# Mixing and expert kernel, one core: a first pair of eight plain products, and mixing weights built from a table on the chip

## The chip, the cores and the metric

One Trainium2 chip, one core of it. The metric is the device time of one execution in microseconds (us), lower is better. The kernel before takes 992.26 us, the median of three runs (991.84 to 992.67).

## The reference, cut to what matters

```python
# x (128, 64, 1024), cond (128, 128), all float32
h = gelu(cond @ W0 + b0); h = gelu(h @ W1 + b1)
att = softmax(h @ W2 + b2)                     # (128, 8)
agg_w = einsum('bk,koi->boi', att, weight)     # one 64x64 mixing matrix for each of 128 batches
z = einsum('boi,bih->boh', agg_w, x) + (att @ bias_k)[:, :, None]
base = z @ base_W.T                            # 1024 x 1024
probs = softmax(z @ router_W.T)                # 8 experts, the best 2, renormalised: w_dense
mid = einsum('bsd,edr->bser', z, lora_A) * w_dense[..., None]      # rank 16 for each expert
out = x + base + einsum('bser,erd->bsd', mid, lora_B) * 2
```

## The kernel before, in words

Two batches make a tile of 128 rows, two tiles of such a kind a pair; there are 32 pairs. For a pair, TensorE first mixes: with `mix_w` (128x128, two 64x64 matrices on the diagonal, one for each batch) it multiplies 16 chunks of x into `y_ps` (`mix_chunk`, L476), and VectorE adds the bias and writes `ya` (`add_bias`, L850). `ya` holds four blocks of 128x512: A11, A21 (first half of the columns), A12 and A22 (second half), where the first index is the set of rows and the second the half of the 1024 columns.

The large product with `base_W` is 2x2 blocks of 1024x1024 halves, and each block product would be eight of them. The kernel uses a rule with seven products: GpSimd makes sums of the blocks of `ya` (S1 to S4: L366, L374, L380, L383), and at the start sums of the weights (T1 to T4, from the blocks B11, B12, B21, B22). Every operand, of data and of weights, is split into a high part (ScalarE: `split_high` L711, `take_hi` L658) and the rest (VectorE: `split_low` L859, `take_lo` L802), and a product is three matmuls for each of four chunks: high by high, high by low, low by high. Four of the seven products carry the router and `lora_A` columns beside them (`product_with_side`, L515 and L518: 12 pairs of matmuls of 376 and 272 columns), three don't (`product`, L504: 12 matmuls of 512 columns).

A tile's routing is a chain of twelve small operations on VectorE with one exponential on ScalarE (L864 to L898), which ends in `mid`. TensorE transposes `mid` into `pd` (`transpose_mid`, L526), ScalarE and VectorE split it (L722, L905), and three matmuls for each half of the columns add `mid` times `lora_B` (`up`, L536). The second tile's `mid` of a pair is used in the next pair, inside its first product. Results gather in `out_sb` (VectorE L910, GpSimd L405), and SyncE stores them and loads x and the residual.

The order on each engine is written out by hand (`body` on every engine, semaphores between them); `over_pairs` runs pairs 0 and 1 unrolled, then a loop of two pairs a turn, then the last two unrolled. In the steady pairs the first four products have the 16 mixing chunks of the next pair between their matmuls (`mixed_in`).

The mixing matrices of all batches but the first four come by way of DRAM: eight matmuls over the kernels' weights (`mixing_kernels`, L432) give all 128x4096 values, ScalarE copies them (`take_agg`, L663) into `agg`, one DMA writes `agg` to DRAM, and four DMAs a pair (L268, 16 KB each in pieces of 128 bytes) bring two 64x64 matrices for each tile into `mix_w`. For the first pair alone, VectorE multiplies a table `mix_i` (128x512: 64 outputs by 8 kernels) by the attention weights (L827), sums over the 8 kernels (L831), and ScalarE places the result (`place_mix`, L672).

## Time and profile before

| what | value |
|---|---|
| median of the runs | 992.26 us (991.84 to 992.67) |
| profiled execution | 992.38 us, of which the span from first to last instruction is 990.6 us |
| granted TensorE clock, mean | 0.989 |
| busy: TensorE, VectorE, GpSimd, ScalarE | 963.9, 686.5, 330.5, 208.7 us |
| DMA | 115.00 MB in 64145 packets, 38392 of them under 512 bytes |

A row of the timeline gives the start, the length of one or of several merged operations, the engine, the line and what is written from what, and in brackets the idle time before it with what ended it. PE is TensorE, DVE VectorE, ACT ScalarE, POOL GpSimd, SP SyncE. "x2" on a float32 matmul counts its two passes.

### The profile page before, as it was taken

The numbers are of one execution on the slowest core, as the hardware profiler recorded it, in microseconds if no ns is written. First come the engines' busy times: TensorE is split into PE (matmuls) and PEld (weight loads), VectorE is DVE, ScalarE is ACT, GpSimd is POOL, SyncE is SP. The second block draws the span as 40 slices with busy tenths as digits, with TensorE's granted clock in tenths as the row PEclk, the third lists the DMA queues.
The fourth block names the chain that finished last, engine by engine and source line by source line (L and its number), as shares of the span: only waits on it lengthen the run. The fifth ranks groups of instructions, "written<-read, shape, count | busy, mean of one in ns | idle before, by whom it ended". The sixth has DMA issues, their size and how long they took to land.

```text
span 990.6 us, 17707 instructions
## 1 busy us (share of the span) xinstructions
PE 963.9 (97%) x5742; PEld 882.8 (89%) x5742; DVE 686.5 (69%) x1529; ACT 208.7 (21%) x422; POOL 330.5 (33%) x245
## 2 busy tenths in 40 slices
PE   6788999999999999999999999999999999999998
PEld 4577999999999999999999999999999999999996
DVE  2878676677676667767667776766776766677674
ACT  3432121122211211212121121211212112122120
POOL 4904333322333322333332233333223333223331
PEclk9889999999999999999999999999999999999999
DMA  8324333433423333332343333334333233433311
GB/s 281 100 122 136 103 106 115 135 108 111 128 93 114 120 132 111 112 113 93 114 135 117 116 122 101 105 114 135 109 111 133 90 115 117 134 109 112 120 48 54
DMA packets 64145, 115.00 MB, mean 116 GB/s; under 512 B 38392, under 2 KB 38520, under 8 KB 63480
## 3 DMA queue, kind: packets, MB, share of 16 engines
q1 hardware_dynamic: 63856, 114.76, 35.0%
q8 instruction: 9, 0.15, 0.1%
q10 hardware_dynamic: 272, 0.03, 0.0%
q14 instruction: 8, 0.07, 0.0%
HBM read 79.01 MB, written 35.68 MB: 116 GB/s over the span
## 4 chain that ended last, share of the span: by engine, by line
PE 91%; issue 4%; POOL 2%; DMA 1%; DVE 1%; SPq 0%; POOLq 0%; DVEq 0%
PE pc L504 17%; PE pa L515 13%; PE pb L515 13%; PE y_ps L476 11%; PE pb L518 9%; PE pa L518 9%; PE pd L504 9%; PE pc L536 4%; PE pd L536 4%; DMA c_raw<-in_base_t 1%; PE pd L526 1%; POOL w_raw L360 1%; POOL w_raw L348 1%; POOL lb_lo L395 0%; DVE out_sb L910 0%
## 5 line engine op out<-in xcount | busy, mean ns | idle before, releaser
L405 POOL TENSOR_TENSOR out_sb<-out_sb,u 128x512 f32<-128x512 f32 x96 | 136.4, 1451 | 209.1 <-DVE u L956 209.1
L476 PE MATMUL y_ps<-mix_w,x_sb 128*128 128x128 f32 x1024 | 199.5, 280 | 0.7 <-issue 0.7
L476 PEld LDWEIGHTS y_ps<-mix_w,x_sb 128*128 128x128 f32 x1024 | 171.9, 194 | 17.3 <-issue 3.9
L366 POOL TENSOR_TENSOR ya<-ya 128x512 f32<-128x512 f32 x32 | 42.6, 1331 | 420.7 <-DVE ya L850 420.7
L850 DVE TENSOR_TENSOR ya<-y_ps,bias_sb 128x512 f32<-128x512 f32 x128 | 87.7, 686 | 34.4 <-PE y_ps L476 31.3
L504 PE MATMUL pc<-w_hi,s_hi 128*128 128x512 f32 x256 | 106.8, 417 | 2.9 <-DVE out_sb L910 2.9
L515 PE MATMUL pa<-w_hi,a_hi 128*128 128x376 f32 x256 | 101.5, 397 | 6.2 <-DVE w_lo L802 6.2
L504 PE MATMUL pc<-w_hi,s_lo 128*128 128x512 f32 x256 | 101.2, 395 | 0.0
L504 PE MATMUL pc<-w_lo,s_hi 128*128 128x512 f32 x256 | 100.5, 393 | 0.0
L515 PE MATMUL pa<-w_lo,a_hi 128*128 128x376 f32 x256 | 86.3, 337 | 0.0
L515 PE MATMUL pa<-w_hi,a_lo 128*128 128x376 f32 x256 | 86.2, 337 | 0.0
L715 ACT ACTIVATE exps<-logits,neg_max 128x8 f32<-128x8 f32 x64 | 19.3, 301 | 300.0 <-DVE neg_max L867 300.0
L722 ACT ACTIVATE mid_hi<-pd 128x128 fp32r<-128x128 f32 x64 | 17.7, 277 | 292.1 <-PE pd L526 292.1
L859 DVE TENSOR_TENSOR a_lo<-ya,a_hi 128x512 fp32r<-128x512 f32 x96 | 69.4, 723 | 8.3 <-ACT a_hi L711 8.3
L518 PE MATMUL pa<-w_hi,a_hi 128*128 128x272 f32 x256 | 74.2, 290 | 0.0
L518 PE MATMUL pa<-w_lo,a_hi 128*128 128x272 f32 x256 | 74.2, 290 | 0.0
L518 PE MATMUL pa<-w_hi,a_lo 128*128 128x272 f32 x256 | 74.0, 289 | 0.0
L910 DVE TENSOR_TENSOR out_sb<-pc,out_sb 128x512 f32<-128x512 f32 x96 | 65.7, 684 | 1.0 <-POOL out_sb L405 0.6
L504 PE MATMUL pd<-w_hi,s_hi 128*128 128x512 f32 x128 | 61.6, 481 | 4.4 <-DVE w_lo L802 4.4
L711 ACT ACTIVATE a_hi<-ya 128x512 fp32r<-128x512 f32 x96 | 60.2, 627 | 25.0 <-DVE ya L850 25.0
L504 PEld LDWEIGHTS pc<-w_hi,s_hi 128*128 128x128 f32 x256 | 48.5, 190 | 14.1 <-issue 3.3
L515 PEld LDWEIGHTS pa<-w_hi,a_hi 128*128 128x128 f32 x256 | 49.5, 193 | 9.8 <-issue 7.0
(149 smaller groups left out, 2373.6 us busy)
## 6 DMA issues: line engine op xcount, KB each, us to landing
x_sb<-in_x SPq DMA_DIRECT2D x64, 512.0 KB, 3.4
out_sb<-in_x SPq DMA_DIRECT2D x64, 512.0 KB, 4.3
out<-out_sb SPq DMA_DIRECT2D x64, 512.0 KB, 2.8
bias_sb<-bias_rows SPq DMA_DIRECT2D x62, 64.0 KB, 5.2
agg_rows<-agg SPq DMA_DIRECT2D x1, 2048.0 KB, 9.1
...
```

The source lines that it names most:

```text
L366: nc.gpsimd.tensor_tensor(y_block(0, 1), y_block(0, 1), y_block(0, 0), ALU.subtract).then_inc(s3_set, 1)
L405: nc.gpsimd.tensor_tensor(o, o, u2[:, :], ALU.add).then_inc(done, 1)
L476: mm = nc.tensor.matmul(y_ps[q % 2][:, j * P:(j + 1) * P], x_sb[m][:, c * P:(c + 1) * P], mix_w[m][:, :], start=True, stop=True)
L504: mm = nc.tensor.matmul(to[:, 0:BANK], y[o][:, j * P:(j + 1) * P], w[:, at:at + BANK], start=(begin and j == 0 and n == 0), stop=(j == HAL ...
L515: nc.tensor.matmul(to[:, LEAD:BANK], y[o][:, j * P:(j + 1) * P], w[:, at:at + HEAD], start=start, stop=stop, skip_group_check=True)
L518: mm = nc.tensor.matmul(to[:, BANK:BANK + 2 * SD].rearrange("p (a n) -> p a n", a=2), y[o][:, j * P:(j + 1) * P], tail, start=start, stop= ...
L536: mm = nc.tensor.matmul(to[:, :], m[:, :], w[:, cols], start=(begin and n == 0), stop=(n == 2), skip_group_check=True)
L711: nc.scalar.activation(op_hi[o][:, :], OPERAND[o], ACT.Copy).then_inc(op_hi_set[o], 1)
L715: nc.scalar.activation(exps[:, :], logits[:, :], ACT.Exp, bias=neg_max[:, :]).then_inc(exps_ready, 1)
L850: nc.vector.tensor_tensor(to[:, :, :, m, :], y_ps[q % 2][:, :].rearrange("p (j s r) -> p j s r", j=HALF, s=2), bias_sb[m][:, :].rearrange( ...
L859: nc.vector.tensor_tensor(op_lo[o][:, :], OPERAND[o], op_hi[o][:, :].bitcast(f32), ALU.subtract).then_inc(op_lo_set[o], 1)
L910: nc.vector.tensor_tensor(o, src, o, ALU.add).then_inc(done, 1)
```

## The change

The first pair no longer uses the seven-product rule: its four blocks are made with eight products (`first_pair` on TensorE: A11 and A21 by B11, A12 and A22 by B21, A11 by B12, A12 by B22, A21 by B12, A22 by B22), so it needs neither the sums of its data nor T1 to T4. Its mixing chunks for the second pair, its two transposes of `mid` and all four `up` steps lie inside it, so the second pair has none of the `up` steps of a pair before it. T1 to T4 are all made by GpSimd, in quarters of 128x512, for the second pair.

The mixing matrices no longer come from DRAM. One matmul of 512 columns puts the attention weights of all tiles on every partition (`att_rows`). For each later tile one operation multiplies the table `mix_i` by them (`scale_mix`), VectorE sums over the 8 kernels (`sum_mix`), and ScalarE places the result with two copies (`place_mix`). For tiles of the second and third pair VectorE multiplies too; from there on GpSimd does. `mixing_kernels`, `take_agg`, `agg` and its DMAs are gone, the start's loads have another order, and the idle transposes of the start are replaced by float32r matmuls of 512 columns (`hot`). The steady pairs' products on TensorE stay as they were.

Cut to its core:

```diff
             sp.dma_start(mlp[:, :], params).then_inc(params_in, 16)
-            sp.dma_start(b2_sb[:, :], b2.partition_broadcast(P)).then_inc(b2_in, 16)
+            sp.dma_start(mix_i[:, :], mix_t).then_inc(mix_i_in, 16)
+            sp.dma_start(bk_sb[:, :], bias_k).then_inc(bk_in, 16)
             sp.dma_start(a_raw[:, :], base_t[0, :, :]).then_inc(a_in, 16)
-            for b in range(PAR):
-                sp.dma_start(mix_i[b * C:(b + 1) * C, :], mix_t).then_inc(mix_i_in, 16)
-            sp.dma_start(bk_sb[:, :], bias_k).then_inc(bk_in, 16)
-            for m in range(2):
-                sp.dma_start(x_sb[m][:, :], x_t[m, :, :]).then_inc(x_in[m], 16)
-            sp.dma_start(mix_k[:, :], mix_rows).then_inc(mix_k_in, 16)
+            sp.dma_start(x_sb[0][:, :], x_t[0, :, :]).then_inc(x_in[0], 16)
             sp.dma_start(w_raw[W_SIDE], side).then_inc(side_in, 16)
+            sp.dma_start(x_sb[1][:, :], x_t[1, :, :]).then_inc(x_in[1], 16)
+            sp.dma_start(b_raw[:, :], base_t[2, :, :]).then_inc(b_in, 16)
             sp.dma_start(c_raw[:, :], base_t[1, :, :]).then_inc(c_in, 16)
             sp.dma_start(d_raw, base_t[3, :, :]).then_inc(d_in, 16)
-            sp.dma_start(b_raw[:, :], base_t[2, :, :]).then_inc(b_in, 16)
             sp.dma_start(lb_raw[:, :], lora_b.rearrange("e r d -> (e r) d")).then_inc(lb_in, 16)
...
-            def mixing_weights(t, m, rows):
-                for b in range(PAR):
-                    dst = mix_w[m][b * C:(b + 1) * C, :].rearrange("i (s b c) -> i s b c", s=2, b=PAR)
-                    r = PAR * t + b
-                    if rows is agg:
-                        src = agg[r:r + 1, :].rearrange("b (i s c) -> b i s c", i=C, s=2)
-                    else:
-                        src = agg_dram[r, :].rearrange("(i s c) -> i s c", i=C, s=2)
-                    sp.dma_start(dst[:, :, b, :], src).then_inc(mix_w_in[m], 16)
+                             ).then_inc(bias_in[m], 16)
...
+            def make_t3(n):
+                nc.gpsimd.tensor_tensor(w_raw[t_piece(T3, n)], c_raw[quarter(n)], w_raw[t_piece(B22, n)],
+                                        ALU.subtract).then_inc(t3_made, 1)
...
+            def scale_mix(n, m, to):
+                pool.wait_ge(summed_set, 2 * n + m)
+                nc.gpsimd.tensor_tensor(to[:, :].rearrange("p (c k) -> p c k", k=K),
+                                        mix_i[:, :].rearrange("p (c k) -> p c k", k=K),
+                                        att_rows[:, bass.ts(2 * n + m, K)].unsqueeze(1).broadcast_to([P, C, K]),
+                                        ALU.mult).then_inc(scaled_set, 1)
...
             def body(p, k):
+                if mixes_after(p):
+                    pool.wait_ge(op_lo_set[S1], p)
+                    scale_mix(p + 2, 0, s1)
                 if not last(p):
-                    sums(p + 1)
+                    sum_s3(p + 1)
+                if mixes_after(p):
+                    scale_mix(p + 2, 1, s1)
...
-                    nc.tensor.transpose(pb[:, 0:P], ident[:, :], ident[:, :])
-            def mixing_kernels(n):
...
+                    nc.tensor.matmul(pb[:, 0:BANK], hot[:, 0:P], hot[:, :], start=True, stop=True)
...
             pe.wait_ge(att_t_ready, 1)
             nc.tensor.matmul(bias_ps, att_t[:, :], bk_sb[:, :], start=True, stop=True).then_inc(bias_mm, 1)
+            keep_warm(1)
...
-                if q < 3:
-                    mixing_kernels(q + 1)
-            pe.wait_ge(agg_act, 2)
-            pe.wait_ge(side_lo_set, 1)
+                if q == 1:
+                    pe.wait_ge(spread_set, 1)
+                    nc.tensor.matmul(pb[:, BANK:], parity[:, :], att_spread[:, :], start=True,
+                                     stop=True).then_inc(att_rows_mm, 1)
...
+            def plain(hi, lo, high_w, low_w, to, j, begin):
+                cols = slice(j * BANK, (j + 1) * BANK)
+                for n, (y, w) in enumerate(((hi, high_w), (hi, low_w), (lo, high_w))):
+                    mm = nc.tensor.matmul(to[:, 0:BANK], y[:, j * P:(j + 1) * P], w[:, cols],
+                                          start=(begin and j == 0 and n == 0), stop=(j == HALF - 1 and n == 2),
+                                          skip_group_check=True)
+                return mm
...
+                for j in range(HALF):
+                    wait_low(w_lo_set[B11], j)
+                    plain_with_side(*a11, B11, pa, j, 0, True)
+                pe.wait_ge(a21_hi_set, 1)
+                pe.wait_ge(a21_lo_set, 1)
+                pe.wait_ge(att_rows_set, 1)
+                for j in range(HALF):
+                    plain_with_side(*a21, B11, pb, j, 0, True)
+                wait_operand(A12, 0)
+                for j in range(HALF):
+                    wait_low(w_lo_set[B21], j)
+                    mm = plain_with_side(*a12, B21, pa, j, 1, False)
+                mm.then_inc(c11_mm, 1)
+                wait_operand(A22, 0)
+                for j in range(HALF):
+                    mm = plain_with_side(*a22, B21, pb, j, 1, False)
+                    if j == HALF - 1:
+                        mm.then_inc(c21_mm, 1)
+                    mix_chunk(1, 0, j)
+                for j in range(HALF):
+                    wait_low(b12_lo_set, j)
+                    mm = plain(*a11, *b12, pc, j, True)
+                    if j == HALF - 1:
+                        mm.then_inc(p1_mm, 1)
+                    mix_chunk(1, 1, j)
+                transpose_mid(0)
+                for j in range(HALF):
+                    wait_low(w_lo_set[B22], j)
+                    mm = plain(*a12, *b22, pc, j, False)
+                    if j == HALF - 1:
+                        mm.then_inc(p2_mm, 1)
+                    mix_chunk(1, 2, j)
+                pe.wait_ge(lb_lo_set, 1)
+                wait_mid(0)
+                plain_up_base(0, pa)
+                up(1, pc, False, plain_up)
+                transpose_mid(1)
+                for j in range(HALF):
+                    mix_chunk(1, 3, j)
+                wait_mid(1)
+                for j in range(HALF):
+                    mm = plain(*a21, *b12, pd, j, True)
+                mm.then_inc(a21_mm, 1)
+                for j in range(HALF):
+                    mm = plain(*a22, *b22, pd, j, False)
+                mm.then_inc(p4_mm, 1)
+                plain_up_base(0, pb)
+                up(1, pd, False, plain_up)
...
+            def place_mix(n, m):
+                act.wait_ge(summed_set, 2 * n + m + 1)
+                if first(n):
+                    act.wait_ge(zeros_set, 4)
+                else:
+                    act.wait_ge(mixed, 4 * n + m - 1)
...
+                if mixes_after(p):
+                    for m in range(2):
+                        place_mix(p + 2, m)
...
+            def sum_mix(n, m, of):
+                dve.wait_ge(scaled_set, 2 * n + m + 1)
+                if not first(n):
+                    dve.wait_ge(mix_set[m], PAR * n)
+                nc.vector.tensor_reduce(summed[m][:, :], of[:, :].rearrange("p (c k) -> p c k", k=K), AX.X,
+                                        ALU.add).then_inc(summed_set, 1)
...
+            def first_pair():
+                add_bias(0, 0)
+                add_bias(0, 1)
+                split_low(A11, 0)
+                low_side()
+                dve.wait_ge(a21_hi_set, 1)
+                nc.vector.tensor_tensor(a21_lo[:, :], y_block(0, 1), a21_hi[:, :].bitcast(f32),
+                                        ALU.subtract).then_inc(a21_lo_set, 1)
+                add_bias(0, 2)
+                add_bias(0, 3)
+                split_low(A12, 0)
+                split_low(A22, 0)
                 for n in range(WP):
                     take_lo(B21, n)
-                dve.wait_ge(t3_made, WP)
+                dve.wait_ge(att_rows_set, 1)
+                for m in range(2):
+                    scale_mix(1, m, scaled)
+                    sum_mix(1, m, scaled)
+                dve.wait_ge(t1_made, TP)
+                dve.wait_ge(t3_made, TP)
                 for n in range(WP):
-                    take_lo(T3, n)
-                dve.wait_ge(t2_made, WP)
-                for n in range(WP):
-                    take_lo(T1, n)
-                dve.wait_ge(p2_mm, 1)
+                    dve.wait_ge(b12_hi_set, n + 1)
+                    nc.vector.tensor_tensor(b12_lo[half_block(n)], c_raw[half_block(n)],
+                                            w_hi[w_piece(T4, n)].bitcast(f32), ALU.subtract).then_inc(b12_lo_set, 1)
+                dve.wait_ge(c11_mm, 1)
                 route_logits(0, pa[:, SLOG])
                 route_choice(0)
                 route_weigh(0, pa[:, SMID])
-                split_low(S2, 0)
-                dve.wait_ge(t4_made, WP)
+                dve.wait_ge(t2_made, TP)
+                for n in range(WP):
+                    take_lo(B22, n)
+                add_bias(1, 0)
+                dve.wait_ge(lb_hi_set, 1)
+                nc.vector.tensor_tensor(lb_lo[:, :], lb_raw[:, :], lb_hi[:, :].bitcast(f32),
+                                        ALU.subtract).then_inc(lb_lo_set, 1)
+                dve.wait_ge(c21_mm, 1)
+                route_logits(1, pb[:, SLOG])
+                route_choice(1)
+                route_weigh(1, pb[:, SMID])
+                split_mid(0)
+                add_bias(1, 1)
+                for n in range(WP):
+                    take_lo(T3, n)
+                split_low(A11, 1)
+                add_bias(1, 2)
+                dve.wait_ge(plain_up, 2)
+                dve.wait_ge(res_in[0][0], 16)
+                add_into(0, 0, 0, pa[:, BASE], plain_out)
+                split_mid(1)
+                add_into(0, 0, 1, pc[:, :], plain_out)
+                split_low(S3, 1)
+                add_bias(1, 3)
+                for n in range(WP):
+                    take_lo(T1, n)
+                split_low(A12, 1)
+                for m in range(2):
+                    scale_mix(2, m, scaled)
+                    sum_mix(2, m, scaled)
+                dve.wait_ge(t4_made, TP)
                 for n in range(WP):
                     take_lo(T2, n)
-                add_p7(0, 0)
-                split_low(S1, 0)
-                make_u2(0)
-                split_low(A22, 0)
-                for n in range(WP):
-                    take_lo(T4, n)
-                split_mid(0)
-                add_bias(1, 0)
...
+                if mixes:
+                    sum_mix(p + 2, 0, s1)
...
+                if mixes:
+                    sum_mix(p + 2, 1, s1)
                 make_u2(p)
                 if mixing:
```

In `body`, GpSimd's queue in the loop. Before, one pair:

```order
L366 TENSOR_TENSOR ya<-ya 128x512 [waits y_ready]
L403 ISA [waits out22_p7,u2_ready]
L405 TENSOR_TENSOR out_sb_73<-out_sb_73,u_77 128x512 [waits res_in01]
L405 TENSOR_TENSOR out_sb_72<-out_sb_72,u_77 128x512 [waits res_in00]
L405 TENSOR_TENSOR out_sb_73<-out_sb_73,u_77 128x512 [waits res_in01]
```

and in the change (`s_56` is S1's buffer, which the products of the table borrow):

```order
L416 TENSOR_TENSOR s_56<-mix_i,att_rows 128x512
L389 ISA
L390 TENSOR_TENSOR ya<-ya 128x512 [waits y_ready]
L415 REGISTER_ALU
L416 ISA [waits summed_set]
L416 TENSOR_TENSOR s_56<-mix_i,att_rows 128x512
L426 ISA [waits out22_p7,u2_ready]
L428 TENSOR_TENSOR out_sb_73<-out_sb_73,u_77 128x512 [waits res_in01]
```

One product stands ahead of the sum S3 (L390) and one right behind it, ahead of the three additions into `out_sb`.

VectorE's queue in the loop, in the change, between the first tile's routing and `u2`:

```order
L1049 TENSOR_TENSOR mid<-pa,gate 128x128 [waits mid_tr,route_step]
L1010 TENSOR_TENSOR a_lo<-ya,a_hi 128x512 [waits op_hi_set0]
L1086 ISA [waits p7_mm]
L1061 TENSOR_TENSOR out_sb_73<-pb,out_sb_73 128x512 [waits res_in01]
L984 REGISTER_ALU
L1001 TENSOR_TENSOR ya<-y_ps,bias_sb_80 128x4x2x64 [waits op_lo_set6,op_lo_set2,mixed]
L1010 TENSOR_TENSOR s_lo<-ya,s_hi 128x512 [waits op_hi_set3]
L928 REGISTER_ALU
L931 TENSOR_REDUCE summed_103<-s_56 128x64 [waits mix_set1,scaled_set]
L1096 TENSOR_TENSOR u_77<-pd,p_76 128x512 [waits u2_in21,p1_kept,p6_mm]
```

The second sum over kernels (L931) is new, right ahead of `u2` (L1096); the first one stands behind the rests of A22 and S4.

TensorE's queue in the first pair, in the change, where A11 by B12 ends and A12 by B22 begins:

```order
L496 MATMUL y_ps<-mix_w_79,x_sb_54 128x128
L569 MATMUL pd<-ident,mid 128x128 [waits route_step]
L561 MATMUL pc<-w_hi,a_hi 128x512 [waits w_lo_set6]
L561 MATMUL pc<-w_lo,a_hi 128x512
L561 MATMUL pc<-w_hi,a_lo 128x512
L496 MATMUL y_ps<-mix_w_78,x_sb_53 128x128 [waits y_ready]
```

The transpose of the first tile's `mid` (L569) stands ahead of the sixth product, and waits for the whole routing chain.

## Rows read from the trace of the kernel before

**Rows 1.** The page's part 1: busy time of each engine.
```profile
PE 963.9 (97%) x5742; PEld 882.8 (89%) x5742; DVE 686.5 (69%) x1529; ACT 208.7 (21%) x422; POOL 330.5 (33%) x245
```
**Rows 2.** Chain of work that ended last: start, us, what (the ends of two pairs).
```profile
113.06 0.70 PE pc L536 x3
...
957.83 0.70 PE pc L536 x3
```
**Rows 3.** Windows: length, busy time of PE, PEld, DVE, ACT, POOL, PEclk, DMA share, GB/s.
```profile
15.00:31.00 16.00, 16.00 (x46) 9.80 (x45) 4.29 (x5) 4.79 (x10) 8.37 (x5) 1.00 0.62 246
31.00:46.00 15.00, 8.82 (x36) 6.34 (x36) 14.14 (x7) 10.42 (x14) 15.00 (x7) 0.81 0.35 114
56.00:83.50 27.50, 20.76 (x99) 17.98 (x100) 20.85 (x40) 9.01 (x14) 5.42 (x4) 0.81 0.11 35
500.00:529.13 29.13, 29.13 (x180) 27.01 (x180) 20.40 (x48) 5.85 (x12) 9.42 (x7) 1.00 0.36 115
```
**Rows 4.** Waits of TensorE: us in total, times, longest.
```profile
PE pa L515 <- DVE w_lo L802: 6.2, 1, 6.2
PE pd L504 <- DVE w_lo L802: 4.4, 1, 4.4
PE pa L432 <- DMA mix_k<-in_mix_rows: 3.5, 1, 3.5
PE pc L504 <- DVE out_sb L910: 2.9, 1, 2.9
```
**Rows 5.** Timeline of TensorE, 0 to 90 us.
```profile
14.02 2.07 PE L432 MATMUL pa<-mix_k,att_t 8*128 8x512 f32 x2 [3.53 <-DMA mix_k<-in_mix_rows]
16.02 1.97 PE L459 MATMUL pd<-bias_rows_sb,pick_row 128*128 128x64 f32 x8
17.78 2.02 PE L476 MATMUL y_ps<-mix_w,x_sb 128*128 128x128 f32 x8
...
31.47 0.66 PE L515 MATMUL pa<-w_hi,a_hi 128*128 128x376 f32 x1
...
33.24 0.44 PE L515 MATMUL pa<-w_hi,a_hi 128*128 128x376 f32 x1
...
83.58 0.34 PE L515 MATMUL pa<-w_hi,a_hi 128*128 128x376 f32 x1
```
**Rows 6.** Timeline of VectorE, 0 to 90 us.
```profile
11.10 0.69 DVE L831 TENSOR_REDUCE summed<-scaled 128x64 f32<-128x512 f32 x1
...
32.47 5.68 DVE L920 TENSOR_TENSOR w_raw<-c_raw,w_raw 128x1024 f32<-128x1024 f32 x2
...
58.47 2.35 DVE L802 TENSOR_TENSOR w_lo<-w_raw,w_hi 128x1024 fp32r<-128x1024 f32 x2
```
**Rows 7.** Timeline of GpSimd, 0 to 90 us.
```profile
18.42 2.35 POOL L348 TENSOR_TENSOR w_raw<-c_raw,a_raw 128x1024 f32<-128x1024 f32 x1 [2.24 <-DMA c_raw<-in_base_t]
...
37.02 6.09 POOL L360 TENSOR_TENSOR w_raw<-b_raw,w_raw 128x1024 f32<-128x1024 f32 x2
```
**Rows 8.** Timeline of VectorE in one steady pair, 500 to 530 us.
```profile
504.14 1.19 DVE L876 TENSOR_TENSOR beats<-ties,earlier 128x64 f32<-128x64 f32 x1
...
510.82 0.69 DVE L956 TENSOR_TENSOR u<-pd,p 128x512 f32<-128x512 f32 x1 [1.29 <-PE pd L504]
...
517.81 0.73 DVE L864 COPY logits<-side_b 128x8 f32<-128x8 f32 x1
...
521.95 0.68 DVE L910 TENSOR_TENSOR out_sb<-pd,out_sb 128x512 f32<-128x512 f32 x1
```
**Rows 9.** Timeline of GpSimd in that pair.
```profile
503.92 1.33 POOL L366 TENSOR_TENSOR ya<-ya 128x512 f32<-128x512 f32 x1 [13.22 <-DVE ya L850]
...
517.22 1.29 POOL L380 TENSOR_TENSOR s<-s,ya 128x512 f32<-128x512 f32 x1
```
**Rows 10.** Timeline of TensorE in that pair: two transposes of `mid`.
```profile
512.92 0.27 PE L526 MATMUL pd<-ident,mid 128*128 128x128 f32 x1
...
523.65 0.27 PE L526 MATMUL pd<-ident,mid 128*128 128x128 f32 x1
```

547 lines of the change are left out of this document (297 added, 250 removed).

## The prediction

> **What bounds the kernel now.** I read the busy times first, then the chain of waits, then the windows, then the timelines of the first 90 us. TensorE is busy 97% of the span and VectorE 69% [rows 1]. The chain shows the same step, the last `up` of a pair, at 113.06 and at 957.83 us, 29 pairs apart: (957.83 - 113.06) / 29 = 29.13 us a pair [rows 2]. The window over one such pair has TensorE busy for all of its 29.13 us at the high clock, 2.4 GHz (granted clock 1.00) [rows 3]. So a steady pair is TensorE's own work, and no change in it helps unless matmuls go; there the change takes none away. What can be won lies ahead of 113.76 us, where the third pair begins. The second pair begins at 83.58 us [rows 5], so the start and the first pair take almost three pairs' time. There TensorE waits 3.5 us for `mix_k`, 6.2 us for the low part of B21, 4.4 us for that of T2 and 2.9 us for an addition into `out_sb` [rows 4]; between 31 and 46 us VectorE is busy 14.1 of 15 us and GpSimd all 15 [rows 3]. The first pair is bound by these two, which make sums and low parts of weights.
>
> **The start.** Before, TensorE waits for `mix_k` until 14.02 us, then runs the first of its matmuls (2.07 us), the eight passes of the bias (1.97 us), and four blocks of mixing of 2.02 us with three more `mix_k` matmuls between them, up to 31.47 us [rows 5]. The change drops these four and the wait. The matmul before the wait ends at 14.02 - 3.53 = 10.5 us; ScalarE's copy of the bias rows puts the bias passes at 11.0. Then come 1.97 us for them, about 0.9 for two wake-up matmuls (estimate, 1024 columns at 1.2 GHz), 8.1 for mixing, and 2.07 for the matmul that spreads the attention weights (512 columns of float32, as `mix_k`). The first product starts at about 24.0 us, 7.5 earlier. Its low parts are not later: the second block of mixing is done at 18, and VectorE needs three operations after it.
>
> **The first pair on TensorE.** It has the work of a steady pair, 29.13 us, plus one product without side columns (12 matmuls at 0.70 / 3 = 0.23 us [rows 2], 2.8 us), plus 0.4 us for `up` steps cut in two: 32.3 us at the high clock. Of it 13.7 us stand behind the first transpose of `mid`: three products (8.3), four `up` steps (3.2), and half of the mixing (eight chunks; four take 2.02 us at 1.2 GHz [rows 5], so 2.0 at 2.4) with a transpose (0.2). So 18.6 us stand ahead of it, and TensorE could be there at 24.0 + 18.6 + 0.9 (the first chunk runs at the low clock, 31.47 to 33.24 [rows 5]) = 43.5 us.
>
> **The first pair on VectorE, which I take to set its time.** A low part of 1024 columns takes 2.35 / 2 = 1.18 us alone and 5.68 / 2 = 2.84 us beside GpSimd's sums, and such a sum takes 2.35 alone and 3.05 beside VectorE [rows 6, 7]. So the two slow each other when both read operands in SBUF. The change gives GpSimd 16 sums of 512 columns (about 1.2 us alone, half of 2.35) without a pause from when B12 lands, near 18 us as before [rows 7], to about 45 us. I price VectorE's operations beside them at 0.6 + 1.1 = 1.7 us for 512 columns and 1.2 + 1.1 = 2.3 for 1024. From 18.6 us it has, ahead of the end of the first tile's routing: six operations of 512 columns (10.2), five of 1024 or 1088 (11.5: side columns, B21, B12), two bias additions and two sums over kernels (2.6; 0.69 each [rows 6]), and the routing (2.6 alone, 5 with waits). That is 29.3 us: `mid` is ready near 48 us, and TensorE, due at 43.5, waits some 4 us in front of the transpose. Behind it VectorE has the low part of B22, a bias addition and lora_B's low part (4.3), the second routing and the first split (2.9), then a bias addition, T3, A11, another bias addition and an addition into `out_sb` (5.4 with one contended), before the second split at about 61 us, for which TensorE waits ahead of the seventh product. Behind that come two products and two `up` steps, 7.1 us. The second pair starts near 67.5 us, with the low clock after the waits in it in part (a window with such waits has a mean of 0.81 [rows 3]).
>
> **The second pair.** 29.13 less two `up` steps and a transpose (1.6) is 27.5 us. Those steps had covered ScalarE's copy of P1, which now stands behind two high parts of T4; I add 1.9 us for it, 0.6 for mixing weights that VectorE finishes late, and 0.7 for the unexplained rest of a first pass through the code. The third pair starts at 98.2 us against 113.76: 15.6 us earlier.
>
> **The steady pairs.** Removed: four DMAs of 16 KB a pair, which nobody waits for. Added on VectorE: two sums of 0.6 us, start to start. Added on GpSimd: two products of 512 columns, no row of their own; S3 is the nearest, 1.33 us [rows 9], and that is my price; the bounds are 1.2 and 2.7 us (twice S3, should the repeated operand halve the rate). ScalarE's four copies fit in its pause (busy 5.85 of 29.13 us [rows 3]). Which waits could become late? The product behind S3 holds VectorE's routing for about 0.65 us more (S3 already holds it: 1.19 us for an operation on 64 columns [rows 8]). With the second sum, `u2` is ready 1.25 us later; before, VectorE stood idle 1.29 us just there [rows 8], so `u2` stays at 511.5 us, and the transpose that needs it runs at 512.92 [rows 10]. The second transpose needs an addition into `out_sb` that ends at 522.6 and runs at 523.65 [rows 8, 10]: slack of 1.0 us. I cost the steady pairs at nothing; the cover is those 1.3 and 1.0 us.
>
> **Sum.** The profiled execution took 992.4 us (span 990.6); less 15.6 is 976.8. The median of the runs is 0.1 lower, so 976.7 us. Differences below 0.2%, 2 us, can't be told from none here.
>
> **A rule against the change.** VectorE's COPY of 8 columns began at 517.81 and took 0.73 us, until 518.54, and GpSimd's sum ran from 517.22 to 518.51 [rows 8, 9]: the copy waited out the whole operation. The Trainium skill (SBUF — State Buffer, Who interferes with whom) has it as an exclusive lock held for a full instruction, and says that `tensor_reduce` never contends on this chip. By that rule the two new sums are free of it, and the first pair's operations wait somewhat longer than my 1.1 us; the sum would come to about 979.
>
> **Rivals.** (1) *Each pair loses (slower).* The product right behind S3 and the second sum delay `u2`, with it GpSimd's three additions and S2, S1, S4, and these then meet the second routing, where S1 and S4 already hold it (0.73 for a copy [rows 8]). Price at the worst: a product of 2.7 instead of 1.33 (+1.4), the sums 1.2, the first product's share 0.65 and one more operation of 1.3 in the second routing, 4.6 us against covers of 1.3 + 1.0: 2.3 us a pair, 67 us over 29 pairs. It decides against the change from 15.6 / 29 = 0.54 us a pair; at 0.8 us a pair the time is 1000. For it speaks that the cover is used up almost exactly; against it that the second cover comes behind the first. Chance 0.07. The first product starts at 18 to 19 us; VectorE then sets the rest, and only 3 to 5 us come of it: 972.5. Chance 0.13. (4) *The start gains, the first pair doesn't*: GpSimd and VectorE block each other for longer (2.8 us for each operation as in [rows 6]): 11 operations by 0.8 more, plus the low clock, 12 us: 989. Chance 0.05. The forecast has 0.58.
>
> **Numbers.** The likely case spans 973 to 980. The range takes in rival 3 and most of rival 2: 970 to 985. Faster by over 0.2%: 0.58 + 0.13 + 0.16 + 0.04 = 0.91; within 0.2%: 0.02; slower: 0.07.
>
> **What would show it.** Right: the first product at 22 to 25 us; the longest waits of TensorE in the first pair in front of the transpose (on `mid`) and of the seventh product (on the low part of `mid`); the second pair at 66 to 69 us, the third at 96 to 100; steady pairs of 29.13 us. Wrong: a steady pair above 29.3 us with TensorE waiting for VectorE, GpSimd's product above 2 us, or a first product at 30 us.

## The result, and the profile after

The changed kernel took 974.95 us, median of 4 runs (974.58 to 976.25), beside 992.46 us of the kernel before in the same job (991.84 to 993.33). The ratio is 0.9825, with a 95% interval from 0.9808 to 0.9842: 17.5 us less, where the prediction had 15.6 less, 976.7 us in a range of 970 to 985. The profiled execution spans 972.9 us, 17.7 less than 990.6.

Busy times of the page, part 1, of the changed kernel:

```profile
PE 953.7 (98%) x5747; PEld 878.3 (90%) x5747; DVE 742.1 (76%) x1592; ACT 231.5 (24%) x537; POOL 402.5 (41%) x305
```

Against [rows 1] VectorE has 55.6 us more to do, GpSimd 72, and the time fell all the same. Where it fell is shown by the chain of waits (start, us, what):

```profile
92.55 2.75 PE pc L524 x12
121.69 2.75 PE pc L524 x12
...
500.37 2.75 PE pc L524 x12
529.51 2.75 PE pc L524 x12
```

From 529.51 back to 121.69 are 14 pairs: 407.82 / 14 = 29.13 us a pair, as in [rows 2]. Nothing was won or lost in the steady pairs. The windows of the first rows' stretches (length, busy time of PE, PEld, DVE, ACT, POOL, PEclk, DMA share, GB/s) show the rest:

```profile
15.00:31.00 16.00, 13.86 (x93) 12.73 (x92) 14.07 (x12) 8.50 (x12) 14.17 (x8) 1.00 0.76 275
31.00:46.00 15.00, 9.91 (x63) 8.97 (x61) 14.59 (x19) 6.13 (x10) 14.43 (x10) 0.99 0.00 1
56.00:83.50 27.50, 24.45 (x142) 22.28 (x142) 26.91 (x42) 8.13 (x16) 9.27 (x6) 0.94 0.52 158
500.00:529.13 29.13, 29.13 (x180) 27.00 (x179) 22.22 (x50) 6.71 (x16) 11.86 (x10) 1.00 0.32 113
```

VectorE now has work for 14.07, 14.59 and 26.91 us of the first three windows; it had it for 4.29, 14.14 and 20.85 [rows 3]. TensorE's longest waits (us in total, times, longest):

```profile
PE pd L569 <- DVE mid L1049: 5.0, 1, 5.0
...
PE pd L561 <- DVE mid_lo L1056: 2.4, 1, 2.4
PE pa L549 <- DVE w_lo L914: 1.1, 1, 1.1
...
PE pa L535 <- ACT p L834: 0.7, 1, 0.7
```

The waits for `mix_k`, for T2 and for the addition into `out_sb`, and most of that for B21 [rows 4], are gone. In the first pair there stand in their place 5.0 us in front of the first transpose of `mid` and 2.4 in front of the seventh product. The timeline of TensorE over the same stretch as [rows 5]:

```profile
13.66 2.53 PE L496 MATMUL y_ps<-mix_w,x_sb 128*128 128x128 f32 x16
16.02 1.02 PE L506 MATMUL pb<-att_spread,parity 128*128 128x512 f32 x2
16.88 1.95 PE L496 MATMUL y_ps<-mix_w,x_sb 128*128 128x128 f32 x16
19.76 0.41 PE L549 MATMUL pa<-w_hi,a_hi 128*128 128x376 f32 x1 [0.93 <-DVE w_lo L976]
...
45.84 0.47 PE L569 MATMUL pd<-ident,mid 128*128 128x128 f32 x1 [5.01 <-DVE mid L1049]
...
58.60 0.47 PE L561 MATMUL pd<-w_hi,a_hi 128*128 128x512 f32 x1 [2.38 <-DVE mid_lo L1056]
```

The first product starts at 19.76 us (31.47 before), the second pair at 67.3 (83.58 before), the third at 95.8, where before it was 113.6. Behind that start both profiled executions have the same length, 972.9 - 95.8 = 877.1 and 990.6 - 113.6 = 877.0 us. So all of the gain lies ahead of the third pair: 11.7 us in the start, 4.5 in the first pair, 1.5 in the second.

Behind each of the two waits the granted clock was low for some time: 0.50 from 46 to 52 us, 0.59 from 58.6 to 62.4. The window:

```profile
46.00:52.00 6.00, 5.25 (x14) 3.66 (x15) 5.70 (x15) 1.91 (x4) 0.00 (x0) 0.50 0.01 1
```

Three matmuls of 512 columns and a mixing chunk took 1.70 us there (49.16 to 50.86) and 0.92 at 1.00 (37.83 to 38.75). So a wait costs more than its own length: some 2.3 us more for the first one, by an estimate from three such groups at 0.78 us each.

What holds TensorE up is seen on VectorE, the routing of the first tile:

```profile
38.35 1.04 DVE L1024 TENSOR_TENSOR beats<-logits 128x64 f32<-128x64 f32 x1
39.31 1.32 DVE L1025 TENSOR_TENSOR ties<-logits 128x64 f32<-128x64 f32 x1
40.67 1.19 DVE L1027 TENSOR_TENSOR beats<-ties,earlier 128x64 f32<-128x64 f32 x1
```

These work on 64 columns and take 0.2 us when nothing else runs. GpSimd was adding up T2 and T4 then, in pieces of 1.2 to 1.9 us. The whole routing took 7.7 us, from 38.1 to 45.8, and the second tile's, from 49.7 with GpSimd idle, 2.6.

### The profile page after: what moved, and what is told of

It is laid out like the page before. It is cut to its first block, busy times and chain, and to the rows that moved or that the text cites. A ratio compares the mean times of both kernels' runs of the same rounds, so it can differ in the third digit from the quotient of the medians.

```text
span 972.9 us, 17928 instructions
## 1 busy us (share of the span) xinstructions
PE 953.7 (98%) x5747; PEld 878.3 (90%) x5747; DVE 742.1 (76%) x1592; ACT 231.5 (24%) x537; POOL 402.5 (41%) x305
## 4 chain that ended last, share of the span: by engine, by line
PE 94%; DVE 5%; issue 1%; ACT 0%; POOL 0%; DVEq 0%; POOLq 0%; ACTq 0%
PE pc L524 17%; PE pa L535 13%; PE pb L535 13%; PE y_ps L496 11%; PE pb L538 10%; PE pa L538 10%; PE pd L524 9%; PE pd L579 4%; PE pc L579 4%; DVE w_lo L914 1%; PE pd L561 1%; PE pd L569 1%; DVE a_lo L1010 0%; DVE b_lo L1136 0%; DVE ya L1001 0%
## 5 line engine op out<-in xcount | busy, mean ns | idle before, releaser
L428 POOL TENSOR_TENSOR out_sb<-out_sb,u 128x512 f32<-128x512 f32 x93 | 132.2, 1451 | 171.8 <-DVE u L1096 171.8
L496 PE MATMUL y_ps<-mix_w,x_sb 128*128 128x128 f32 x1024 | 194.9, 275 | 0.2
L496 PEld LDWEIGHTS y_ps<-mix_w,x_sb 128*128 128x128 f32 x1024 | 168.2, 190 | 13.1 <-DVE ya L1001 0.8
L416 POOL TENSOR_TENSOR s<-mix_i,att_rows 128x512 f32<-128x512 f32 x58 | 74.6, 1286 | 164.4 <-DVE s_lo L1010 164.4
L390 POOL TENSOR_TENSOR ya<-ya 128x512 f32<-128x512 f32 x31 | 42.2, 1362 | 198.9 <-DVE ya L1001 198.9
L524 PE MATMUL pc<-w_hi,s_hi 128*128 128x512 f32 x248 | 102.4, 413 | 0.0
L535 PE MATMUL pa<-w_hi,a_hi 128*128 128x376 f32 x248 | 97.8, 394 | 0.7 <-ACT p L834 0.7
L524 PE MATMUL pc<-w_hi,s_lo 128*128 128x512 f32 x248 | 97.5, 393 | 0.0
L524 PE MATMUL pc<-w_lo,s_hi 128*128 128x512 f32 x248 | 96.9, 391 | 0.0
L535 PE MATMUL pa<-w_lo,a_hi 128*128 128x376 f32 x248 | 82.8, 334 | 0.0
L1078 DVE TENSOR_TENSOR side_b<-pb,p 128x136 f32<-128x136 f32 x31 | 9.3, 300 | 65.8 <-PE pb L538 65.8
## 6 DMA issues: line engine op xcount, KB each, us to landing
b_raw<-in_base_t SPq DMA_DIRECT2D x1, 1024.0 KB, 11.5
```

Of the source, the lines that this page charges most:

```text
L390: nc.gpsimd.tensor_tensor(y_block(0, 1), y_block(0, 1), y_block(0, 0), ALU.subtract).then_inc(s3_set, 1)
L416: nc.gpsimd.tensor_tensor(to[:, :].rearrange("p (c k) -> p c k", k=K), mix_i[:, :].rearrange("p (c k) -> p c k", k=K), att_rows[:, bass.ts ...
L428: nc.gpsimd.tensor_tensor(o, o, u2[:, :], ALU.add).then_inc(done, 1)
L496: mm = nc.tensor.matmul(y_ps[q % 2][:, j * P:(j + 1) * P], x_sb[m][:, c * P:(c + 1) * P], mix_w[m][:, :], start=True, stop=True)
L524: mm = nc.tensor.matmul(to[:, 0:BANK], y[o][:, j * P:(j + 1) * P], w[:, at:at + BANK], start=(begin and j == 0 and n == 0), stop=(j == HAL ...
L535: nc.tensor.matmul(to[:, LEAD:BANK], y[o][:, j * P:(j + 1) * P], w[:, at:at + HEAD], start=start, stop=stop, skip_group_check=True)
```

## The experiments

Twelve kernels ran. The theory (A): VectorE's queue sets the time of the first two pairs, GpSimd's sums hold it, and the steady pairs have a cover that the new work fits in. The rivals: TensorE's own work sets it; each half of the change brings its own part; a steady pair sits on an edge.

The ratios are to the kernel before in the same job (medians of 992.46 to 993.23 us). Where the third pair starts is the reading I use, since all that follows is 877 us in every one of the kernels with steady pairs unchanged. The first product of the profiled executions came at 19.5 to 22.8 us, although nothing before it differs between most of these kernels. Part of a late start is made up for: in e7, which is the changed kernel up to the second pair, it came 2.8 us later and the third pair 1.3. So a place in one profile is good to about a microsecond, and the medians of the runs decide.

| run | time, us (runs) | ratio, 95% | third pair at |
|---|---|---|---|
| before | 992.46 (4) | | 113.6 |
| changed kernel | 974.95 (4) | 0.9808 to 0.9842 | 95.8 |
| e1_t4_late | 973.41 (5) | 0.9794 to 0.9821 | 94.7 |
| e2_t3_late | 975.73 (5) | 0.9818 to 0.9845 | 96.0 |
| e3_both_late | 975.37 (5) | 0.9813 to 0.9839 | 96.9 |
| e4_table_only | 990.35 (9) | 0.9967 to 0.9987 | 111.0 |
| e5_transposes | 974.82 (5) | 0.9804 to 0.9831 | 95.6 |
| e6_pool_twice | 975.26 (5) | 0.9807 to 0.9834 | 95.6 |
| e7_dve_products | 975.48 (5) | 0.9805 to 0.9832 | 97.1 |
| e8_dve_three | 992.56 (10) | 0.9986 to 1.0005 | 96.4 |
| e9_lo_by_act | 972.20 (4) | 0.9773 to 0.9806 | 93.9 |
| e10_lo_by_act_t4_late | 969.08 (4) | 0.9742 to 0.9775 | 91.4 |
| e11_weights_early | 973.62 (4) | 0.9791 to 0.9823 | 94.5 |
| e12_weights_on_act | 972.37 (5) | 0.9781 to 0.9808 | 93.7 |

### GpSimd's hold on the routing: e1_t4_late

```diff
-            pool.wait_ge(b_in, 16)
-            for n in range(TP):
-                make_t4(n)
...
                 sum_s3(1)
+                pool.wait_ge(b_in, 16)
+                for n in range(TP):
+                    make_t4(n)
                 sum_s2(1)
```

> The changed kernel, with GpSimd's four T4 sums moved from before to behind the second pair's S3. In the changed kernel VectorE's first routing took 7.7 us (38.1 to 45.8), its second, with GpSimd at rest, 2.6 us, and TensorE waited 5.0 us for `mid` at the first transpose. Theory A (GpSimd's sums hold VectorE, and the first pair waits for VectorE): the first routing takes 3 us or less, the wait at the transpose is under 2 us, the third pair starts 1 to 4 us before 96.0, and the time is 971 to 974 us. It is not the whole 5 us, because the sums then run beside the second pair's low parts, which VectorE owes TensorE too. Rival B (the routing waits for something else, the exponents or the semaphores' own latency): routing still 6 us or more, wait still about 5 us, 975 us. Rival C (the first pair is bound by TensorE's own work, its waits only take turns): routing short, wait gone, but the third pair at 96 and 975 us.

Measured: 973.41 us, third pair at 94.7. VectorE's routing, in its timeline, where GpSimd's last T2 sum ended at 41.4:

```profile
40.43 1.04 DVE L1024 TENSOR_TENSOR beats<-logits 128x64 f32<-128x64 f32 x1
41.39 0.21 DVE L1025 TENSOR_TENSOR ties<-logits 128x64 f32<-128x64 f32 x1
41.64 0.23 DVE L1027 TENSOR_TENSOR beats<-ties,earlier 128x64 f32<-128x64 f32 x1
```

and TensorE's waits behind it:

```profile
43.63 0.33 PE L569 MATMUL pd<-ident,mid 128*128 128x128 f32 x1 [0.74 <-DVE mid L1049]
...
57.43 0.47 PE L561 MATMUL pd<-w_hi,a_hi 128*128 128x512 f32 x1 [4.21 <-DVE mid_lo L1056]
```

The same instruction, `ties`, took 1.32 us beside GpSimd's sum and 0.21 without. The routing took 3.4 us (one operation of it still held; 3 or less were expected) instead of 7.7, and the wait at the transpose fell from 5.0 to 0.7 us. Only about half of these 4.3 us is the move's: this execution's first product came at 21.82, 2.1 us later than the changed kernel's, and `mid` was done 2.2 us sooner (43.6 against 45.8). e3, which has the same move and started at 19.48, is the cleaner reading: its routing took 4.5 us (37.8 to 42.3), and `mid` was 3.4 us sooner. That is theory A; B falls. But the wait at the seventh product grew from 2.4 to 4.2, since the sums now run beside the low parts of T3 and A11, and 1.5 us came off the time.

### The second wait: e2_t3_late, e3_both_late and e11_weights_early

```diff
-                for n in range(WP):
-                    take_lo(T3, n)
                 split_low(A11, 1)
...
                 split_mid(1)
                 add_into(0, 0, 1, pc[:, :], plain_out)
+                for n in range(WP):
+                    take_lo(T3, n)
                 split_low(S3, 1)
```

The two halves of T3's low part leave their place ahead of A11's. e3 has this and the move of e1; e11 has both and the third pair's mixing weights ahead of the low parts of T3.

> The changed kernel, with VectorE's two low parts of T3 moved behind the split of the second tile's transposed middle and the last addition that goes with it. In the changed kernel TensorE waited 2.4 us there, at the seventh product, for `mid_lo`. If that wait is a loss of its own: the wait goes and the time falls by 2 us, to 973. If VectorE's whole queue bounds the first two pairs: the wait goes, the second pair starts about 2 us sooner, at 65, and waits there for what VectorE now gives it later (low parts, the third pair's mixing weights, p1): third pair at 95.5 to 96.5, time within 1 us of 975.

> Both moves of the two runs beside this one in one kernel. If waits add up: 5 us less, 970. If VectorE's queue is the bound of the first two pairs, the first pair ends 5 to 8 us sooner (second pair at 60 to 62) and a new wait of 3 to 5 us stands at the start of the second pair, for the third pair's mixing weights (summed behind all low parts) and for p1: third pair at 94 to 96.5, time 973 to 975.5.

Measured: 975.73 and 975.37 us. In e2 the wait at the seventh product fell to 0.4 us and the second pair began at 63.5 instead of 67.3, yet the third began at 96.0: TensorE now waited 2.8 us for the third pair's mixing weights and 1.6 for ScalarE's copy of P1. In e3, by TensorE's timeline, both waits have shrunk to 1.8 and 0.6 us and a third has come:

```profile
42.39 0.33 PE L569 MATMUL pd<-ident,mid 128*128 128x128 f32 x1 [1.84 <-DVE mid L1049]
...
53.11 0.47 PE L561 MATMUL pd<-w_hi,a_hi 128*128 128x512 f32 x1 [0.58 <-DVE mid_lo L1056]
...
66.53 0.77 PE L496 MATMUL y_ps<-mix_w,x_sb 128*128 128x128 f32 x2 [5.28 <-issue]
```

The 5.28 us, for which the profile names no engine, stand at the first matmul that needs the third pair's mixing weights, which VectorE sums behind the low parts of T3, S3, T1 and A12. The second pair began at 60.2 instead of 67.3, and all 7.1 us were paid back, and one more: the third began at 96.9, past the 96.5 expected. The new wait had its low clock too (0.55 from 66.5 to 73 us). e11 asks whether those weights alone are late.

> The kernel with both moves (T4 sums late, low parts of T3 late), which waited 5.3 us at the third pair's first mixing matmul, with the third pair's mixing weights multiplied and summed on VectorE ahead of the low parts of T3, S3, T1 and A12 and placed ahead of A12's high part. If those weights were the whole wait: it goes, third pair at 89 to 91, 969 us. If VectorE's queue is the bound whatever its order: the wait goes there and comes again at the low parts that now stand behind (A12 or p1), third pair at 94 to 96, 973 to 976 us.

Measured: 973.62 us, third pair at 94.5. The wait for the weights is gone and the second pair begins at 60.7. TensorE now waits at the second product of that pair, for ScalarE's copy of P1:

```profile
69.16 0.41 PE L535 MATMUL pa<-w_hi,a_hi 128*128 128x376 f32 x1 [3.80 <-ACT p L834]
```

That copy stood behind the high parts of S1 and T4, and these behind GpSimd's sums for the second pair, which began at 61.38, when VectorE had written the last block of `ya`. The chain of waits runs through VectorE, over the low parts of weights:

```profile
57.37 2.73 DVE w_lo L914 x2
62.36 2.30 DVE w_lo L914
67.40 2.29 DVE w_lo L914
74.59 2.27 DVE w_lo L914 x2
```

VectorE was busy for all but 0.03 us from 56 to 70; of the four orders tried, the best two won 1.3 and 1.5 us (e11, e1).

### Is it VectorE's amount of work: e9_lo_by_act and e10_lo_by_act_t4_late

```diff
+                    nc.scalar.activation(w_lo[w_piece(blk, n)], w_raw[w_piece(blk, n)], ACT.Copy
+                                         ).then_inc(w_lo_set[blk], 1)
...
-                    take_lo(T3, n)
```

(for T3, T1, T2 and T4 alike; e10 has the move of e1 as well.) What stands in for the low part is the sum itself, and the subtraction is left out: these two kernels measure what VectorE's queue is worth and are no versions to use. ScalarE also copies P1 first in the second pair, so that its new work doesn't delay that.

> The changed kernel, with the low parts of T3, T1, T2 and T4 (eight pieces of 128x1024) taken off VectorE: ScalarE, which is mostly idle, writes the sums themselves there, by copy, and keeps p1 first in the second pair. So the low part is not the difference, and the products take wrong numbers, but TensorE's and GpSimd's work is the same. VectorE is rid of 9 to 11 us between 51 and 78 us. Theory A (VectorE's queue bounds the first two pairs): the wait of 2.4 us at the seventh product goes, the second pair starts near 65 (67.3), and the third at 92 to 94 (96.0), so 971 to 973 us; the 5.0 us at the first transpose stay, since they lie ahead of it. Rival B (it is TensorE's own work, or ScalarE's and GpSimd's): third pair at 95.5 to 96.5, 975 us.

> The kernel beside this one, with GpSimd's T4 sums behind the second pair's S3 as well (the same wrong low parts). Theory A (VectorE's queue, and GpSimd's hold on it): both waits go, which together were 7.4 us, and here nothing is given back, since VectorE has room: second pair at 61 to 63, third pair at 89 to 91, 968 to 970 us. Rival B: as in the first of the four experiments, where the same move gave 1.5 us: third pair no more than 1.5 us ahead of the run beside this one.

Measured: 972.20 and 969.08 us, third pair at 93.9 and 91.4. TensorE's waits in e10:

```profile
44.36 0.33 PE L569 MATMUL pd<-ident,mid 128*128 128x128 f32 x1 [0.51 <-DVE mid L1062]
...
55.08 0.47 PE L561 MATMUL pd<-w_hi,a_hi 128*128 128x512 f32 x1 [0.47 <-DVE mid_lo L1069]
```

Nothing was taken from TensorE or GpSimd, so rival B (TensorE's own work, or GpSimd's) falls. Both profiled executions started late, with first products at 22.74 and 22.80; in e9 the wait at the first transpose was 3.4 us for that reason, not the 5.0 expected. With VectorE relieved, the same move of T4's sums is worth 3.1 us (972.20 to 969.08) instead of 1.5. Both times lie within what theory A had expected; e10's third pair is 0.4 us later than the 89 to 91.

### The two halves of the change: e4_table_only

The kernel before with the table, its products and sums, and without mixing kernels and their DMAs:

```diff
-            pe.wait_ge(mix_k_in, 16)
-            mixing_kernels(0)
...
-                if q < 3:
-                    mixing_kernels(q + 1)
+                if q == 1:
+                    pe.wait_ge(spread_set, 1)
+                    nc.tensor.matmul(pb[:, BANK:], parity[:, :], att_spread[:, :], start=True,
+                                     stop=True).then_inc(att_rows_mm, 1)
```

> The kernel before, with one half of the change: mixing weights from the table (multiplied on VectorE for the second and third pair, on GpSimd from the fourth, summed on VectorE, placed by ScalarE), no mixing kernels, no rows through DRAM; the first pair still by the seven products. TensorE's wait for `mix_k` and eight matmuls go, so its first product starts at 21 to 25 us, against 31.47 before. Theory A (that earlier start is worth nothing without the plain first pair, since T3, T1, T2, T4 and their low parts stand in front of the second to sixth product): TensorE waits 6 to 12 us more at B21 and T2, the third pair starts at 112 to 115 (before 113.76), time 990 to 994. Rival B (each half brings its part): the start's 7 to 10 us are kept, third pair at 104 to 107, time 982 to 985. In the steady pairs both expect 29.13 us a pair.

Measured: 990.35 us, ratio 0.9967 to 0.9987, third pair at 111.0. TensorE's timeline:

```profile
20.68 0.41 PE L501 MATMUL pa<-w_hi,a_hi 128*128 128x376 f32 x1 [0.31 <-DVE a_lo L869]
36.16 0.65 PE L501 MATMUL pa<-w_hi,a_hi 128*128 128x376 f32 x1 [11.68 <-DVE w_lo L785]
...
56.70 0.76 PE L490 MATMUL pd<-w_hi,s_hi 128*128 128x512 f32 x1 [10.84 <-DVE w_lo L785]
```

The first product comes 10.8 us earlier than before, and TensorE then waits 11.7 us for B21's low part (6.2 before [rows 4]) and 10.8 for T2's (4.4 before): of 10.8 us, 2.2 reach the time (992.51 to 990.35; third pair at 111.0, a little ahead of the 112 expected). The products by seven need sums of weights whose making bounds the pair, so the early start is worth almost nothing until the first pair needs none. The 15.4 us between e4 and the changed kernel come with the plain first pair. The counterpart, the plain first pair with the old mixing weights, wasn't tried, so how much of them needs the early start as well is not shown.

### The start: e5_transposes

```diff
-                    nc.tensor.matmul(pb[:, 0:BANK], hot[:, 0:P], hot[:, :], start=True, stop=True)
+                    nc.tensor.transpose(pb[:, 0:P], ident[:, :], ident[:, :])
```

> The changed kernel, with the float32r matmuls of 512 columns that TensorE runs while it has nothing to do put back to transposes of 128 columns, as before. In the changed kernel the granted clock was at 2.4 GHz when mixing began, at 13.66 us, and 16 mixing matmuls took 2 us; before, at 1.2 GHz, they took 4 to 5. Theory A (VectorE's queue bounds the first two pairs): the clock is low in the mixing, the first product starts later than 19.76 by 1 to 4 us, but what follows waits less at B21, the transpose and the seventh product, and the third pair starts at 96 to 97.5: time 975 to 976.5. Rival B (the time of the first pair is TensorE's): first product at 24, third pair at 99 to 100, time 978 to 979. Rival C (those matmuls don't set the clock): the mixing stays at 2.4 GHz.

Measured: 974.82 us, third pair at 95.6. Mixing in TensorE's timeline:

```profile
13.04 2.85 PE L496 MATMUL y_ps<-mix_w,x_sb 128*128 128x128 f32 x16
16.59 1.95 PE L496 MATMUL y_ps<-mix_w,x_sb 128*128 128x128 f32 x16
```

Rival C came true: 16 mixing matmuls take 1.95 us with and without the float32r matmuls, where 8 took 2.02 before [rows 5]. So it makes no difference here which of the two kinds TensorE runs while it idles (a kernel with neither wasn't run). What the expectation calls 1.2 GHz before is TensorE's speed there, not the granted clock, which was 1.00 (last section). A and B couldn't be told apart, as the start didn't move; e9 and e10 did that.

### The cover of the steady pairs: e6_pool_twice, e7_dve_products and e8_dve_three

In their order: one more product on GpSimd, both products moved to VectorE (the second one shown), three more sums on VectorE.

```diff
+                    nc.gpsimd.tensor_tensor(s2[:, :], mix_i[:, :], mix_i[:, :], ALU.mult).then_inc(again_set, 1)
```

```diff
-                if mixes_after(p):
-                    scale_mix(p + 2, 1, s1)
                 add_u2(p, k)
...
                 if mixes:
+                    scale_mix(p + 2, 1, s1)
                     sum_mix(p + 2, 1, s1)
```

```diff
+                    for n in range(3):
+                        nc.vector.tensor_reduce(again[:, n * 32:(n + 1) * 32],
+                                                s1[:, :].rearrange("p (c k) -> p c k", k=16), AX.X, ALU.add
+                                                ).then_inc(again_set, 1)
```

> The changed kernel, with one more product of 128x512 on GpSimd in each pair from the second on, right behind the second one (the table by itself, into s2, which is free then). It ends 3.8 us before GpSimd is wanted for the additions of u2, so GpSimd's own queue has room for it. Theory A (each such product holds VectorE for up to its 1.3 us, and `u2` has 1.4 us to spare: it was ready at 522.9 and TensorE read past it at 524.3): `u2` is ready 0.7 to 1.3 us later, TensorE doesn't wait, 29.13 us a pair, 975 us. Rival B (the slack is smaller than it looks, or other work of VectorE's falls late): 0.2 to 1 us a pair, 981 to 1003 us.

> The changed kernel, with both products of each steady pair on VectorE, in front of their sums, and none on GpSimd. VectorE gets 2 x 0.68 us more to do a pair, and is no longer held by GpSimd's product at `beats` (1.20 against 0.23) and at `chosen` (0.83 against 0.17), so `u2` is ready up to 0.9 us sooner or at most 0.1 later. Theory (there is 1.4 us to spare before `u2` and GpSimd's products gained nothing in the steady pairs): 29.13 us a pair, 975 us. Rival (the work had to leave VectorE, which is busy without a gap from 514.5 to 524.1 of a pair): 0.2 to 0.7 us a pair, 981 to 995 us.

> The changed kernel, with three more sums of 128x512 on VectorE in each pair (each into a place of its own that nobody reads), right in front of `u2`. One takes 0.68 us and the next starts 0.60 us behind it, so `u2` comes 1.8 us later, at 524.7 of the pair where TensorE wants it at 524.3. Theory (1.4 us of slack and no more): TensorE waits for `u2` 0.4 to 0.6 us in each of some 28 pairs, 986 to 992 us, 29.5 to 29.7 us a pair. Rival (what slips here is made up for within the pair): 975 to 977 us. Rival (other work queued behind it on VectorE falls late as well, the low part of the next pair's second operand among it): over 30 us a pair, above 1000 us.

Measured: 975.26, 975.48 and 992.56 us. First the changed kernel, VectorE in a steady pair, beside [rows 8]:

```profile
518.05 0.17 DVE L1037 TENSOR_TENSOR picked<-exps,chosen 128x8 f32<-128x8 f32 x1
...
521.52 0.68 DVE L931 TENSOR_REDUCE summed<-s 128x64 f32<-128x512 f32 x1
522.19 0.69 DVE L1096 TENSOR_TENSOR u<-pd,p 128x512 f32<-128x512 f32 x1
```

and the transpose that needs `u2`, on TensorE:

```profile
524.29 0.27 PE L569 MATMUL pd<-ident,mid 128*128 128x128 f32 x1
```

The 1.29 us that VectorE stood idle in front of `u2` [rows 8] are used up, and `u2` still ends 1.4 us ahead of the transpose, as before (510.82 + 0.69 = 511.51 against 512.92 [rows 8, 10]). In e6 the third product holds one more operation:

```profile
517.85 0.87 DVE L1042 TENSOR_TENSOR picked<-exps,chosen 128x8 f32<-128x8 f32 x1
...
522.62 0.68 DVE L1101 TENSOR_TENSOR u<-pd,p 128x512 f32<-128x512 f32 x1
```

`picked` takes 0.87 instead of 0.17 us; `u2` starts 1.48 us ahead of its transpose (at 524.10) instead of 2.10, and the pair stays at 29.13. In e7 the start is 2.10 again (523.48 and 525.58): the first product falls into time in which VectorE had been idle (0.95 us left of 1.68 ahead of the second routing), and what the second one costs, it gets back at `chosen`, which takes 0.17 us instead of 0.83. Having the products on GpSimd brought the steady pairs nothing. Nor do they explain that e7's third pair starts 1.3 us late: TensorE is late already at its wait for P1 (73.90 against 72.62), before VectorE's first such product at 78.20, and from there to the third pair both take 23.2 us. This profiled execution had its first product at 22.53, 2.8 us late. In e8 the edge is reached, by its chain and its list of waits:

```profile
122.99 2.75 PE pc L527 x12
152.69 2.75 PE pc L527 x12
```

```profile
PE pd L572 <- DVE u L1099: 7.5, 29, 0.5
```

29.70 us a pair there, and 16.1 us more span over some 28 pairs, 0.57 each, where 1.8 us more work in front of 1.4 of slack had let 0.4 to 0.6 be expected; the median is 0.6 us above the 992 expected. The list puts only 7.5 us down to `u2`, 0.25 a pair, because it counts idle time from the modelled end of the matmul before:

```profile
502.92 0.40 PE L527 MATMUL pc<-w_hi,s_lo 128*128 128x512 f32 x1
503.56 0.32 PE L572 MATMUL pd<-ident,mid 128*128 128x128 f32 x1 [0.25 <-DVE u L1099]
```

Here the transpose starts 0.64 us behind the start of that matmul, in the changed kernel 0.23 (524.06 to 524.29). So the wait costs 0.41 us a pair; the remaining 0.16 isn't settled.

### A version that beats both: e12_weights_on_act

```diff
+                    for k in range(K):
+                        mm = nc.scalar.activation(to[:, :].rearrange("p (c k) -> p c k", k=K)[:, :, k],
+                                                  mix_i[:, :].rearrange("p (c k) -> p c k", k=K)[:, :, k], ACT.Copy,
+                                                  scale=att_rows[:, (2 * n + m) * K + k:(2 * n + m) * K + k + 1])
```

This kernel also has both moves of e3, and T2's low parts stand behind two additions.

> The kernel with both moves (T4 sums late, low parts of T3 late), and the mixing weights of the second and third pair multiplied on ScalarE, in 8 activations of 64 columns for a tile, each with its attention column as the scale, while ScalarE is idle (31 to 35 and 41 to 48 us); VectorE only sums them, and those of the third pair are placed ahead of A12's high part. VectorE is rid of 5.4 us of products and waits for them (1.77 and 0.94 us twice in the run with late T4 sums) that GpSimd held. Theory A (VectorE's queue bounds the first two pairs, so work that leaves it comes off the time): third pair at 91.5 to 93.5, 970.5 to 972.5 us, below the changed kernel and below the best order of it so far (973.4). Rival B (ScalarE becomes late instead, at the second pair's high parts and p1, or the order of the outputs costs what is saved): third pair at 94 to 96, 973 to 975 us.

Measured: 972.37 us, ratio 0.9781 to 0.9808; its five runs (971.98 to 972.68) all lie below the changed kernel's four, as do those of e1 (973.30 to 973.45). They come from different jobs, though, and by the intervals of the ratios e12 just touches the changed kernel (0.9808 to 0.9842), while e1 (0.9794 to 0.9821) overlaps with it, so e1's lead is not beyond doubt. Against e3, which has the same two moves without ScalarE's products, it is 3.0 us faster; T2's place differs too. The third pair starts at 93.7, a little later than expected (91.5 to 93.5), and TensorE's timeline has a wait left for the third pair's weights:

```profile
64.49 0.46 PE L497 MATMUL y_ps<-mix_w,x_sb 128*128 128x128 f32 x2 [2.88 <-issue]
```

ScalarE had had those products ready since 47.8, but VectorE summed them at 63.17, behind T1's low parts. 16 such activations took 5.06 us on ScalarE, where VectorE had needed 1.77 + 0.94 for its two products; but ScalarE was idle. VectorE stood idle for 1.5 and 1.7 us ahead of the second pair's two sums, which need them (for the second wait the profile names ScalarE).

## Why the prediction was right, and where not

**The bound and its place: right.** All 17.5 us came ahead of the third pair, and VectorE with GpSimd set the first pair (e9, e10). VectorE's queue up to `mid` was put at 29.3 us from 18.6; it ran from 17.6 to 45.8, 28.2 us. The two longest waits of the first pair stood where they were expected, 5.0 and 2.4 us.

**The size of that queue: close by luck.** Its terms were off both ways. Six operations of 512 columns took 7.9 us, not 10.2, since not all were held; five of 1024 or 1088 took 9.7, not 11.5 (B21's low parts at 4.54 / 2 = 2.27 us met the price of 2.3, those of B12 took 1.9, the side columns 1.28). The routing took 7.7, not 5: with operations this small nearly the whole length is waiting, and that was undersized. One row was also misread on the way: the 5.68 us of [rows 6] are two sums of weights for T3 (L920), not low parts, of the same width. The second pair's start, put at 67.5 and measured at 67.3, is luck of the same kind: the second split came at 58.4, not 61, and the two products and two `up` steps behind it took 8.7 us (58.60 to 67.32), not 7.1, at a granted clock of 0.59 for the first 3.8 us.

**The start: wrong by 4.2 us**, 19.76 against 24.0, outside the 22 to 25 that were to show it right. The failed terms are the 8.1 us for mixing, which took 2.53 + 1.95 = 4.5, and the 2.07 for the spreading matmul, which took 1.02 (a wait of 0.9 for the side columns' low part gave some of it back): I had carried the speed of [rows 5] over. Rival 3 had nearly this start (18 to 19), and named the float32r matmuls as its cause; e5 shows that they are not. It did little harm to the sum for the reason that the prediction gave: VectorE, not TensorE, sets the end of the first pair.

**The second pair: 30.7 us expected, 28.5 measured**, and this is the whole net error of the sum. The terms for ScalarE's late copy of P1 (1.9), late mixing weights (0.6) and an unexplained rest (0.7) were 3.2 us; what showed was one wait of 0.7 for P1, and no wait for weights. T4's high parts were no hindrance: ScalarE was through with them at 69.8 and stood idle 2.0 us before P1's product ended, and the 0.7 is about the copy's own length (0.71).

**The steady pairs: right**, with the terms near their sizes: the product took 1.29 us (mean of 58; price 1.33, bounds 1.2 to 2.7). The cover in front of `u2` was read as 1.3 us of idle time with 1.25 used; behind it lay 1.4 us more, down to the transpose, which [rows 8, 10] had shown and the prediction had not counted; e8 confirms 1.2 to 1.4. So rivals 1 and 2 were further off than their chances of 0.07 and 0.17 say.

**The rule on the shared lock: the trace agrees.** `ties` took 1.32 us beside a GpSimd sum, 0.21 without, and while GpSimd ran one sum after the other, from 18.92 to 41.39, e1's VectorE timeline has

```profile
32.30 1.77 DVE L921 TENSOR_TENSOR scaled<-mix_i,att_rows 128x512 f32<-128x512 f32 x1
34.10 0.69 DVE L931 TENSOR_REDUCE summed<-scaled 128x64 f32<-128x512 f32 x1
```

a product held for 1.1 us and a reduction of as many columns that took the 0.69 of [rows 6]. The exclusive lock of the Trainium skill (SBUF — State Buffer, Who interferes with whom) describes both. Its 979 us did not come: the longer wait that it gives did show in the routing (7.7 against 5), but the price of 1.1 us for each larger operation already had the lock in it (2.27 measured, 2.3 priced) and was too high for those that were not held.
